# Expert, router and value biases taken out of TensorE's inner products, one product of routing weights and biases put in, and the engines' orders written anew

## The reference, cut to what matters

```
x = x + tanh(g_xattn[0]) * attention_0(ln(x), ctx)             # 16 heads of 8, softmax over 1601 keys
x = x + tanh(g_ffn[0])   * experts_0(ln(x))                     # "v"
x = x + tanh(g_xattn[1]) * attention_1(ln(x), ctx)              # only the 32 greatest of 1601 scores a row
x = x + tanh(g_ffn[1])   * (self_attention(ln(x)) + experts_1(ln(x)))   # "z"

experts_0: scores = x @ Wr + br; w = softmax over the 2 greatest of 8, else 0
           out = sum_e w[e] * (gelu(x @ W1[e] + b1[e]) @ W2[e] + b2[e])      # 8 experts, 512 hidden
experts_1: gate = softmax(x @ W_gate + b_gate); w = its 2 greatest, else 0
           out = sum_e w[e] * (x @ W_experts[e] + b_experts[e])              # 8 experts
self_attention: v = x @ W_v + b_v; its softmax weights sum to 1 in each row
```

## Time and profile before

| what | value |
|---|---|
| median of 3 executions | 5390.07 us (5384.35 to 5394.43) |
| span of the profiled execution | 5390.7 us |
| TensorE busy (products) | 4654.8 us, 86% |
| VectorE busy | 4315.2 us, 80% |
| ScalarE busy | 4029.9 us, 75% |
| GpSimd busy | 1153.0 us, 21% |
| mean granted TensorE clock | 0.945 |

### The profile page before, as it was taken

How to read it: one execution, slowest core, us unless ns; L and a number is a source line. 1 busy time by engine, 2 the same in 40 slices (tenths; PEclk the granted TensorE clock), 3 DMA queues, 4 the chain that set the end, 5 groups by cost and what they waited for, 6 DMA issues and landing times. The chain is left out here.

```text
span 5390.7 us, 109932 instructions
## 1 busy us (share of the span) xinstructions
PE 4654.8 (86%) x34502; PEld 2211.0 (41%) x34502; DVE 4315.2 (80%) x22968; ACT 4029.9 (75%) x5196; POOL 1153.0 (21%) x2648
## 2 busy tenths in 40 slices
PE   4878779999797999889899999997999799988776
PEld 2435235353443535344353534444353444534222
DVE  4457887879888797987988798898879888877772
ACT  1447767879687787868778797886879688886763
POOL 2121112222121222212222222222222122121110
PEclk7889899999998999999999999999999999999886
DMA  4232222223122232322323232221323122121110
GB/s 122 69 77 55 58 62 60 71 58 82 48 72 62 57 71 60 78 53 63 72 52 75 58 75 61 73 70 49 75 56 81 49 64 67 48 57 28 34 24 19
DMA packets 356330, 332.18 MB, mean 62 GB/s; under 512 B 102073, under 2 KB 313148, under 8 KB 355710
## 3 DMA queue, kind: packets, MB, share of 16 engines
q1 hardware_dynamic: 355710, 324.84, 24.8%
HBM read 217.54 MB, written 107.13 MB: 60 GB/s over the span
## 5 line engine op out<-in xcount | busy, mean ns | idle before, releaser
L951 DVE MAX8 cand<-s 128x8 f32<-128x67 f32 (+1 forms) x12288 | 1998.7, 225 | 117.5 <-ACT s L903 68.9
L922 ACT ACTIVATE prob<-wide 128x1024 f32<-128x1024 f32 (+1 forms) x1792 | 1775.3, 1025 | 379.9 <-PE wide L644 181.9
L1037 DVE TENSOR_REDUCE part<-score 128x1 f32<-128x512 f32 x1536 | 1031.8, 683 | 346.7 <-PE score L598 247.6
L690 PE MATMUL att<-prob,v 128*9 128x256 f32 (+1 forms) x14336 | 1104.5, 388 | 27.6 <-ACT prob L922 25.9
L644 PE MATMUL wide<-q,k_att 128*128 128x256 bf16 (+1 forms) x6656 | 1014.3, 279 | 101.5 <-ACT s L903 53.9
L903 ACT ACTIVATE s<-wide 128x1024 f32<-128x1024 f32 (+1 forms) x1024 | 844.4, 846 | 286.2 <-DVEq L1094 149.5
L912 ACT ACTIVATE below<-wide 128x1024 bf16<-128x1024 f32 (+1 forms) x832 | 828.7, 1024 | 131.3 <-PE wide L644 122.6
L644 PEld LDWEIGHTS wide<-q,k_att 128*128 128x128 bf16 (+1 forms) x6656 | 580.8, 100 | 564.7 <-ACT s L903 148.7
L598 PE MATMUL score<-k_scan,q 128*128 128x512 bf16 x1536 | 584.1, 396 | 176.2 <-DVE part L1037 86.0
L1283 POOL TENSOR_SCALAR flag<-cand,ends 128x24 bf16<-128x24 f32 x512 | 177.5, 347 | 2461.7 <-DVE ends L976 2254.9
L666 PE MATMUL wide<-below,minus_ident 128*128 128x512 bf16 (+1 forms) x1664 | 504.5, 386 | 101.8 <-ACT below L912 90.9
(11 more groups left out here) (164 smaller groups left out, 5335.4 us busy)
## 6 DMA issues: line engine op xcount, KB each, us to landing
k_scan<-k_stack SPq DMA_DIRECT2D x512, 150.1 KB, 2.7
k_stack<-split_b SPq DMA_DIRECT2D x576, 128.0 KB, 2.5
k_att<-k_stack SPq DMA_DIRECT2D x384, 192.0 KB, 3.4
ctxT<-in_ctx_dram SPq DMA_DIRECT2D x32, 800.5 KB, 5.6
q_stack<-split_b SPq DMA_DIRECT2D x192, 64.0 KB, 2.1
q<-q_stack SPq DMA_DIRECT2D x128, 96.0 KB
self_stack<-split_b SPq DMA_DIRECT2D x192, 64.0 KB, 2.2
k_self<-self_stack SPq DMA_DIRECT2D x64, 96.0 KB
```

The lines of the kernel that those rows point to most:

```text
L690: r = tensor.matmul(att[32 * j:32 * j + HD + 1, 0:S], v[0:kc, c, j0 * HG + j, :], m.prob[n % 3][0:kc, j * S:(j + 1) * S], start=(c == 0), ...
L922: scalar.activation(pr[0:kc, :], ps[0:kc, :], ACT.Exp, scale=SCALE).then_inc(sem["wide_done"], 1)
L951: i = vector.max(cand[:, :, c], s[:, KCUT[c]:KCUT[c + 1]])
L1037: vector.tensor_reduce(m.part[:, QT * hh + qt, c:c + 1], score[i % 2][:, :], AX.X, ALU.max).then_inc(sem["score_max"], 1)
```

## The change

The bias products of route, v_w2, z_v and z_moe are left out; those of o_proj stay. The routers' biases are loaded to all partitions and added by VectorE as it takes the scores out of PSUM. For each batch and each of the two expert layers, four new steps: rw_turn (TensorE transposes the weights `one`, 128 x 8, twice), rw_copy (ScalarE copies them to mixT), mix_bias (TensorE: weights times biases, 8 or 9 rows, 256 tokens), mix_start (ScalarE copies that to acc, to which all experts now add). The ninth row of layer 1 is ones, against it stands the value bias of self-attention. The cycles of TensorE, ScalarE, VectorE and SyncE are new; GpSimd's is the same. Every LAG but GpSimd's is lower, as the new cycles start at another point: w_k.0 now begins in the first cycle instead of the second, and from there to the last x_add.z the table runs through 19.7 cycles. Scratch for dynamic DMAs is set to 1024.

```diff
-    flag=("small_full", 1), b_o=("small_full", 1), pv=("pv_done", 1), pv_z=("pv_done", 1),
+    flag=("small_full", 1), rw_turn=("small_full", 1), mix_bias=("small_full", 1), b_o=("small_full", 1), pv=("pv_done", 1), pv_z=("pv_done", 1),
...
-    route_exp=("route_exp_done", 1), gates=("gates_done", 1), att_copy=("att_out", 1),
+    route_exp=("route_exp_done", 1), gates=("gates_done", 1), mix_start=("mixed", 1), att_copy=("att_out", 1),
...
     pe="""
-        cut_add c1 pv.1 n0 c1 pv.1 c1 row_turn.0 c1 s_1 n0 s_1 cut_add n0 cut_add w_k.1 pv.1 s_1*2 pv.1 n0*2 cut_add
...
-        ln_turn.v c1*2 route.v s_1*2 n0 cut_add*2 n0 z_moe row_turn.0 s_1 pv.1*2 s_1 z_score n0 cut_add flag cut_add
-        c1 pv.1 z_score c1 pv.1 w_k.0 v_w1*2 n0 z_score s_1 v_w2 s_1 cut_add n0 z_score v_w2 cut_add c1 n0 pv.1 n0
-        flag c1 pv.1 s_1 n0 row_turn.2 c1 cut_add row_turn.1 n0*2 v_w1*2 pv.1 n0*2 c1 v_w2 w_v.0 s_0 v_w2 s_0*2 pv.0
-        flag n0*2 c1 pv.0 u_turn.1 s_0*2 pv.0 n0 ln_turn.w c1 pv.0 v_w1*2 pv.0 n0*2 s_0 v_w2 s_0 n0*2 w_k.0 pv.0 s_0
-        c1 v_w2 s_0 c1 pv.0*2 n0 s_0 pv.0 s_0 n0 z_score v_w1*2 pv.0*2 flag n0 z_score s_0 v_w2 w_q s_0 pv.0 s_z v_w2
...
+        pv.1 w_k.0 rw_turn.v c1 z_score c1 mix_bias.v s_1 n0 v_w2 s_1 n0 cut_add v_w2 cut_add z_score c1*2 flag s_1
+        pv.1 c1 row_turn.2 n0 cut_add n0 pv.1*2 v_w1 n0 v_w1 row_turn.1 n0 pv.1 c1 v_w2 s_0 n0 c1 n0 v_w2 s_0 pv.0
+        n0 s_0 n0 c1 flag pv.0 s_0 w_v.0 n0*2 s_0 v_w1 u_turn.1 n0 v_w1 pv.0*3 ln_turn.w c1 n0 s_0 n0 v_w2 z_score
+        s_0 n0 s_0 pv.0 w_k.0 s_0 pv.0*2 c1 s_0 pv.0 w_q s_0 n0 v_w2 s_0 v_w1*2 pv.0 flag pv.0*2 c1 v_w2 s_0 n0 s_z
+        n0 v_w2 s_z pv.0 s_1 n0 s_1 pv_z*2 cut_add u_turn.0 z_score*2 cut_add w_v.0 z_score c1 u_turn.2 s_1 n0 s_1
...
+        cut_add n0 z_v c1 u_turn.0 w_v.1 n0 c1 o_turn.0 z_qk c1 route.z z_qk n0 c1 s_1 n0 s_1 pv.1*2 n0 cut_add*2 n0
+        o_proj.0 w_v.1 s_1 n0 s_1 pv.1 cut_add n0 flag cut_add rw_turn.z z_moe mix_bias.z c1 pv.1 ln_turn.v n0*2
+        c1*3 route.v s_1*2 pv.1 row_turn.0 n0 cut_add pv.1 cut_add z_moe s_1 z_score s_1 pv.1 cut_add pv.1 cut_add
+        v_w1 n0 z_score flag n0 v_w1 n0""",
...
     act="""
...
+        exp_1 v_gelu*2 rw_copy.v w_k_out.0 c1_out mix_start.v cut c1_out cut exp_1*2 c1_out*2 cut row_minus.2 exp_1
+        c1_out v_gelu row_minus.1 v_gelu c1_out exp_0 att_copy.1 c1_out exp_0*2 c1_out exp_0 w_v_out.0 exp_0
+        v_gelu*2 ln_copy.w c1_out exp_0*3 w_k_out.0 exp_0 c1_out exp_0 w_q_out exp_0*2 v_gelu*2 c1_out exp_0 exp_z*2
...
+        c1_out cut*2 route_exp.z exp_1*2 w_v_out.1 cut*2 exp_1 rw_copy.z exp_1 z_moe_out mix_start.z c1_out
+        ln_copy.v c1_out*3 cut*2 exp_1*2 z_moe_out cut*2 row_minus.0 exp_1 route_exp.v""",
     dve="""
...
+        v_add ln_stats.w rank ln_aggr.w n0_max rank n0_max v_add rank n0_max*2 check n0_max*3 o_norm.1 ln_scale.w
+        rank*2 n0_max rank n0_max v_add rank z_max rank n0_max rank*2 v_add n0_max check v_add n0_max rank n0_max
...
     sp="""
-        k_scan.1 k_att.0 rows_out.0 rows_in.0 k_scan.0 split_out.w_k.1 k_att.0 k_scan.1 k_att.0 q_in.1 k_att.0
-        k_scan.0 k_scan.1 k_att.1 rows_out.1 rows_in.1 k_att.1 q_in.0 k_att.1 k_scan.0 k_scan.1 k_att.1 split_out.z_qk
...
+        kq_in*2 x_in k_att.0 ctx_in.0 k_scan.1 k_scan.0 rows_out.0 k_att.1 k_scan.0 q_in.1 rows_in.0 rows_out.1
+        k_scan.1 k_scan.0 k_att.0 rows_out.2 k_att.1 rows_in.1 rows_in.2 split_out.w_k.0 k_att.1 k_att.0 k_scan.1
+        k_scan.0 split_out.w_k.0 kq_in q_in.0 k_att.1 rows_out.2 k_scan.1 k_scan.0 k_att.1 split_out.w_q k_att.0
+        rows_out.0 k_att.0 k_scan.0 k_scan.1 rows_in.0 rows_in.2 split_out.w_k.0 rows_out.2 k_att.0 rows_in.2
...
+        "rw_turn.v": 2, "mix_bias.v": 2, "rw_turn.z": 3, "mix_bias.z": 3},
...
-        m.b_rows = sb("b_rows", [65, E * D])
-        one = [m.ones_rows[32 * n:32 * n + 1, :] for n in range(3)]
-        b_2, b_e = m.b_rows[0:1, :], m.b_rows[32:33, :]
+        m.b_rows = sb("b_rows", [65, QT * D])
+        one = m.ones_rows[64:65, :]
         b_o = [m.b_rows[64:65, l * D:(l + 1) * D] for l in range(2)]
-        b_v2 = m.b_rows[64:65, 2 * D:3 * D]
-        b_route = dict(v=m.b_rows[64:65, 3 * D:3 * D + E], z=m.b_rows[64:65, 3 * D + E:3 * D + 2 * E])
+        MIX = dict(v=E, z=E + 1)
+        m.b_mix, m.mixT = {}, {}
+        for n, rows in MIX.items():
+            m.b_mix[n], m.mixT[n] = sb(f"b_mix_{n}", [rows, D]), sb(f"mixT_{n}", [rows, S])
+        m.b_route = dict(v=sb("b_route_v", [P, QT, E]), z=sb("b_route_z", [P, QT, E]))

...
-                  (b_2, a["L0_ffn_b2"].rearrange("(o e) d -> o (e d)", o=1)),
-                  (m.w_r[:, :], a["L0_ffn_Wr"]), (b_route["v"], row("L0_ffn_br")),
+                  (m.b_mix["v"][:, :], a["L0_ffn_b2"]), (m.w_r[:, :], a["L0_ffn_Wr"]),

...
+                  (m.b_mix["z"][0:E, :], a["L1_ffn_b_experts"])]
+        for t in range(QT):
+            loads += [(m.b_route["v"][:, t, :], row("L0_ffn_br").to_broadcast([P, E])),
+                      (m.b_route["z"][:, t, :], row("L1_ffn_b_gate").to_broadcast([P, E]))]

...
+            if name == "rw_turn":
+                return "rw_copy", key
+            if name == "mix_bias":
+                return "mix_start", key
...
                     elif name == "route":

...
                         for t in range(QT):
-                            tensor.matmul(ps[:, t * E:(t + 1) * E], m.xnT[kind][:, t * P:(t + 1) * P], w_route[kind][:, :],
-                                          start=True, stop=False)
-                            r = tensor.matmul(ps[:, t * E:(t + 1) * E], one[2], b_route[kind], start=False, stop=True)
+                            r = tensor.matmul(ps[:, t * E:(t + 1) * E], m.xnT[kind][:, t * P:(t + 1) * P], w_route[kind][:, :],
+                                              start=True, stop=True)
+                        r.then_inc(sem["small_full"], 1)
+
+                    elif name == "rw_turn":
+                        kind, b = key
+                        ps = claim(name, *key)
+                        q.wait_ge(sem["routed"], after("route_pick", *key))
+                        for t in range(QT):
+                            r = tensor.transpose(ps[0:E, t * P:(t + 1) * P], m.r[kind].one[:, t, :], m.ident[:, :])
+                        r.then_inc(sem["small_full"], 1)
+
+                    elif name == "mix_bias":
+                        kind, b = key
+                        ps = claim(name, *key)
+                        q.wait_ge(sem["turned"], after("rw_copy", *key))
+                        for t in range(QT):
+                            r = tensor.matmul(ps[:, t * D:(t + 1) * D], m.mixT[kind][:, t * P:(t + 1) * P],
+                                              m.b_mix[kind][:, :], start=True, stop=True)
                         r.then_inc(sem["small_full"], 1)
 

...
                         for t in range(QT):
-                            tensor.matmul(ps[:, t * D:(t + 1) * D], one[0], b_2[:, e * D:(e + 1) * D],
-                                          start=True, stop=False)
                             for k in range(PT):
                                 r = tensor.matmul(ps[:, t * D:(t + 1) * D], hid[:, k, t * P:(t + 1) * P],
-                                                  m.w_2[:, e, k, :], start=False, stop=(k == PT - 1))
+                                                  m.w_2[:, e, k, :], start=(k == 0), stop=(k == PT - 1))

...
                     elif name == "z_v":
                         for t in range(QT):
-                            tensor.matmul(ps[:, t * D:(t + 1) * D], m.xnT["z"][:, t * P:(t + 1) * P], m.w_qkv[:, 2, :],
-                                          start=True, stop=False)
-                            r = tensor.matmul(ps[:, t * D:(t + 1) * D], one[2], b_v2, start=False, stop=True)
+                            r = tensor.matmul(ps[:, t * D:(t + 1) * D], m.xnT["z"][:, t * P:(t + 1) * P],
+                                              m.w_qkv[:, 2, :], start=True, stop=True)

...
                     elif name == "z_moe":
-                            tensor.matmul(ps[:, x:x + BANK], m.xnT["z"][:, t * P:(t + 1) * P], m.w_e[:, x:x + BANK],
-                                          start=True, stop=False)
-                            r = tensor.matmul(ps[:, x:x + BANK], one[1], b_e[:, x:x + BANK], start=False, stop=True)
+                            r = tensor.matmul(ps[:, x:x + BANK], m.xnT["z"][:, t * P:(t + 1) * P], m.w_e[:, x:x + BANK],
+                                              start=True, stop=True)

...
+                    elif name == "rw_copy":
+                        kind, b = key
+                        q.wait_ge(sem["small_full"], after("rw_turn", *key))
+                        q.wait_ge(filled, 6)
+                        if b:
+                            q.wait_ge(sem["small_full"], after("mix_bias", kind, b - 1))
+                        scalar.activation(m.mixT[kind][0:E, :], small[0:E, 0:S], ACT.Copy).then_inc(sem["turned"], 1)
+
```

(38 more changed lines are left out.)

164 lines of the change are left out of this document (76 added, 88 removed), and 6 rows, old and new, of the table sp.

## The result

The changed kernel takes 5033.09 us (median of 4, 5030.98 to 5038.72) against 5387.21 us for the one before on the same chip: a ratio of 0.9343, 95% interval 0.933 to 0.9357. It is 354 us faster. The forecast was 5270 us with a range from 5180 to 5400, so it is missed by 237 us: outside the range, though on the right side of before.

The account below looks back on a forecast made before the run. TensorE was taken as the bound, above all at v_w2, with VectorE nearly as full elsewhere. 3.7 + 3.2 + 0.7 = 7.6 us a cycle, times 16 = 122 us off 5390.7: 5270 us, range 5180 to 5400.

Parts of the forecast that it names:

- The bound: Whole kernel: TensorE is the one waited for, above all at its f32 products; busy 86% of the span.
- The cycle: One batch lasts 320 us, from a 540 us window; sixteen make 5117 us, filling and draining the other 274 us.
- The removal: Bias products of v_w2, z_moe, route, z_v: 12.86 us of TensorE a batch removed, net 10.1 after added steps.
- How much counts: Of 10.1 us, all 3.7 in the 40 us of v_w2 count, and half of the other 6.4, 3.2 us.
- The step that failed: New orders' own gain: 0.7 us a cycle, half of 1.4 us, and none for filling and draining.
- The sign that I had named: Prediction is wrong if the new cycles cost or bring more than 7 us a cycle by themselves.
- the three maxima moved into VectorE's hole: Around v_w2: new order brings three maxima of 0.68 us into VectorE's idle time, one out; 1.4 us, half counted.
- 1, VectorE the bound elsewhere: VectorE binds everywhere outside the 40 us of v_w2; only 3.7 us a cycle count: 60 us, 5330 us; chance 22%.
- 2, the new cycles pay: New cycles fill VectorE's idle time in the v_w2 stretch: 12.6 us a cycle, 200 us, 5190 us; chance 12%.
- 3, SyncE: SyncE's order brings rows_in.1 late for s_1, four times 3.1 us a cycle: +77 us, 5468 us; chance 14%.
- 4, the chain of new steps: Chain route, pick, rw_turn, rw_copy, mix_bias, mix_start makes TensorE stand: no change, about 5388 us; chance 9%.
- 5, the clock: TensorE's clock falls in the v_w2 stretch, 15 us a cycle less 7.6: +115 us, 5505 us; chance 3%.

Follow-up runs that it names:

- the zero products: Changed kernel with bias products put back on a row of zeros: in v_w2 5185.33 us, in z_moe 5120.43 us.
- The biases alone: The changed computation (bias products out, new steps put in) in the old orders of the kernel before: 5259.19 us, 0.9754.
- The orders alone: Kernel before, its computation and bias products kept, with the new ORDER and LAG less the four new steps: 5219.28 us, 0.9689.
- two more pairs: Changed kernel with two more pairs of neighbouring pv steps in TensorE's cycle, 25 instead of 23: 5035.63 us, 0.9342.
- pv paired: Changed computation in the old orders, with 11 places of TensorE's cycle changed so that pv steps stand together: 5276.50 us, 0.9796.
- the short cut: ScalarE's step cut takes 512 of 1024 columns in 252 turns: ratio 0.9934 before, 0.9673 orders only, 0.9664 biases out only, 0.9325 changed kernel.
- the short maxima: VectorE's z_max reads 64 of 256 keys of a row: 5373.16 us in the kernel before, 5011.68 us in the changed kernel.

## Why the prediction was wrong

**The bound** was right. TensorE's work costs more than its price after the change (the zero products). Of VectorE's 101 us 13 to 21 are paid, of ScalarE's 107 only 9 or 10 in the new orders, though 36 and 48 in the old ones. **The cycle** was taken too long: 320 us from one window, where it is 313 from the first v_w2 to the last (4695.2 / 15), so filling and draining were larger than the 274 us put down for them.

**The removal** was mis-sized, low. A v_w2 step is 1.0 us shorter where 0.82 were counted. Counted from the weight loads of all steps, the removed products were worth 15.5 us a batch, not 12.9, and the added steps cost 2.2, not 2.8: net 13.3 against 10.1.

**How much counts** came out near by luck, as two errors cancel. The biases alone bring 129 us, where this part of the sum was 6.9 x 16 = 110 and the whole 122. In the v_w2 stretch, where I took 3.7 us, the relief brings 5.8 in the old orders and 7.3 in the new. A stretch has 7 of the 8 steps, each 1.0 us shorter, so that is four fifths and all of it. Outside, where I took half of 6.4 us, 3.2, the medians show 0.9 in the old orders and 2.7 in the new.

**The step that failed** is the last of the sum: "I count half, 0.7 us" for the new orders, 11 us in all, with "no gain of their own" for filling and draining. Of the 237 us missed, 158 are this term (169 against 11), 56 what orders and relief bring only together, and 19 the relief. The sign that I had named came true: the cycles brought 9.1 us a cycle by themselves, more than 7. The orders alone bring 169 us, in the span 176: 24 before the first v_w2, 136 between, 16 after the last (the three parts of its span, 5215.1). In the stretch where I looked for it, the three maxima moved into VectorE's hole, nothing came: 62.1 against 61.4 us. The 9 us a cycle are in the rest, where I had weighed nothing word by word. The equal number of turns, 19.6 and 19.7, said nothing about filling. Why the first v_w2 comes 24 us earlier is argued, not shown: in the first cycles steps are left out, and it may matter which remain. ORDER and LAG were changed together in every run. From 58 to 400 us, VectorE's wait for n0, before, with SyncE's order alone, and with all new orders:
```profile
DVE part L1037 <- PE score L598: 150.2, 64, 24.4
```
```profile
DVE part L1037 <- PE score L598: 62.2, 45, 4.2
```
```profile
DVE part L1037 <- PE score L598: 34.0, 38, 2.6
```

**What the orders do** can be seen in TensorE's waits. The largest, before:
```profile
PE wide L666 <- ACT below L912: 90.9, 252, 1.1
PE score L598 <- DVE part L1037: 86.0, 89, 19.2
PE score L777 <- DVE mx L1057: 79.9, 20, 23.3
PE wide L644 <- ACT s L903: 53.9, 66, 20.7
PE wide L618 <- ACT prob L922: 52.1, 145, 0.8
PE score L598 <- DVE part L1040: 46.8, 7, 22.0
PE score L598 <- DMA k_scan<-k_stack: 40.5, 5, 20.0
...
PE wide L644 <- ACT prob L922: 34.5, 105, 0.7
```
and after:
```profile
PE wide L676 <- ACT below L949: 70.0, 230, 0.8
...
PE wide L654 <- ACT s L940: 64.2, 63, 22.3
PE score L799 <- DVE part L1074: 47.8, 5, 23.0
PE wide L654 <- DMA q<-rows: 38.8, 16, 3.6
PE score L608 <- DVE part L1074: 32.9, 72, 2.3
PE wide L628 <- ACT prob L959: 26.6, 93, 0.9
PE score L799 <- DVE mx L1094: 24.3, 17, 3.3
```
Summed over all lines, TensorE waits for ScalarE at wide and att 326 us before, 227 with the new orders, 352 with the biases out, 219 with both; for VectorE at score 221, 130, 235 and 137. New waits take some back: at small for VectorE 41 to 114 us with the biases in and 70 to 159 with them out, for row bounds from under 1 to 35 and 39. All waits of TensorE together are 96 us less by the orders with the biases in (706 to 611) and 173 with them out (847 to 674). Missing records lengthen the waits in the last three of these traces. The complete one of the changed kernel with two more pairs has 605 in all, 199 for ScalarE and 139 for VectorE at score; that of the old orders with the biases out and pv paired has 823, 366 and 254. So the new orders let TensorE meet its two partners with fewer stands, above all at prob and at score; this is how the trace looks, and the short cut shows it for ScalarE to the amount of 30 us. Which words of the cycle do it stays open. In the old orders neither the pairing of pv nor holding it back between the cut_adds nor SyncE's order does it by itself. No run exchanges the order of TensorE, ScalarE or VectorE alone, or the LAG alone. Open too is most of the 56 us: the removal pays more in the new orders, seen from both sides (129 us against 186 us), and ScalarE isn't the main reason.

**The rivals.** 1, VectorE the bound elsewhere: refuted by the short maxima (13 us of 101), though in the old orders the biases pay only 18 us outside the stretches. 2, the new cycles pay: the right one, with the wrong mechanism and 5190 us against 5033; the gain isn't in VectorE's hole. 3, SyncE: real in the old orders, 88 us; in the changed kernel 2.4 us once a cycle are seen, not 3.1 four times. 4, the chain of new steps: no, the stand at rw_turn.z is 1.5 us and for another reader. 5, the clock: no. (Its price set a duration at the lower level, 0.74 us, against a distance of starts, 0.41; the duration at the upper level is 0.48.) Windows of 20 us after, columns as in rows 2:
```profile
2240.00:2260.00 20.00, 18.29 (x126) 10.90 (x127) 18.40 (x108) 16.39 (x24) 6.23 (x12) 1.00 0.07 16
2260.00:2280.00 20.00, 19.40 (x159) 13.46 (x160) 17.95 (x97) 17.20 (x30) 3.38 (x9) 1.00 0.11 28
2280.00:2300.00 20.00, 19.68 (x167) 13.96 (x169) 10.72 (x58) 16.38 (x23) 6.90 (x12) 1.00 0.45 117
```
This is a stretch of v_w2 again, and the clock stays at its upper level, 2.4 GHz. TensorE is busy for 18.3 to 19.7 of 20 us, with a few records missing; the complete trace has 18.57, 19.61 and 20.00 in the same windows. So one window of full TensorE is left of the two in the earlier trace rows, and VectorE has 18.4, 18.0 and 10.7.

## What to carry to other kernels

Where the engines' orders are written out, a new order is an edit of its own: time it alone, before its effect is taken for that of the computation it came with. A stretch where one engine never stops tells what its work is worth there; stretches with many short waits have to be weighed apart. There the new orders alone were worth 135 us and the removed work 18, and once the orders were new, a product put back counted there nearly in full. So what a relief is worth depends on the order that it meets. And an order belongs to the others: SyncE's new one costs 88 us in the old surroundings and is part of the changed kernel. A trace with missing records makes an engine look idler than it was: compare the counts of products and weight loads before comparing idle times.

## What the runs showed that I had not expected

An f32 product with one row and 128 columns, ahead of four full ones, costs TensorE 0.50 us (0.56 in the step shown) and not the 0.41 by which they start later; put back, the 256 of them cost the kernel 152 us, 0.59 each, of which the stretches of v_w2 show 0.50. A window of the changed kernel has VectorE in its second search and TensorE nearly idle, with the clock at 0.51, about the lower level of 1.2 GHz, 20 us after 0.93:
```profile
2120.00:2140.00 20.00, 13.07 (x82) 5.06 (x82) 19.18 (x72) 12.67 (x14) 4.16 (x6) 0.93 0.06 12
2140.00:2160.00 20.00, 4.19 (x20) 1.50 (x21) 19.38 (x41) 3.37 (x6) 1.84 (x6) 0.51 0.00 1
2160.00:2180.00 20.00, 18.00 (x146) 7.37 (x147) 18.70 (x105) 18.42 (x23) 2.53 (x10) 1.00 0.36 74
```
The Trainium skill ("TensorE: Matmul & The Clock Gate", Part 1) says that the clock is halved when the engine has been idle. By that rule the trace agrees: the granted clock fell where TensorE was busy for 4.19 of 20 us. The warning on transposes that the prediction weighed did not show: two of the four new transposes of a batch stand in the window from 2240 us above (at 2242.2 and 2242.3 us), and its clock is 1.00. So few of them among so many other products are no hard test of it. The search itself is 32 times 1.83 and 1.81 us of VectorE, in eight places of the run, before and after, 116 us in all, and no kernel here shortened it. The lines of after:
```profile
L1128 DVE MAX8 top_again<-s x32: 1828/1828/1830, 534.9 to 3944.6; 128x8 f32<-128x1601 f32 x32
...
L1125 DVE MATCH_REPLACE8 s<-top_again,s x32: 1811/1812/1815, 536.9 to 3946.6; 128x1601 f32<-128x1601 f32 x32
```
